# A second accumulator that is added whole to the first, in a scatter-add at the end of a mixture-of-experts layer

## The reference

```python
# layer 0: adaLN, causal attention, dense 8-expert feed-forward; layer 1: adaLN, linear attention, then:
t = rms_norm(xf) * norm_w                                   # 2048 rows
vals, idx = top_k(t @ gate_w.T + gate_b, 4)                 # 16 experts, 4 for each token
G = zeros((M, E)).at[arange(M)[:, None], idx].set(softmax(vals))
h = einsum('mh,eoh->emo', t, w1) + b1
a, b = minimum(h[..., ::2], 7), clip(h[..., 1::2], -7, 7)
y = einsum('emi,edi->emd', a * sigmoid(1.702 * a) * (b + 1), w2) + b2
x = x + gb * (x_in + einsum('me,emd->md', G, y))            # four expert results are added to each token's row
```

## Time and profile before

| | us |
|---|---|
| median of three runs (lowest, highest) | 1005.02 (1004.24, 1008.51) |
| time of the profiled execution | 1002.58 |
| its span, first to last instruction | 1000.8 |
| TensorE busy in it | 969.1 (97%) |
| VectorE busy | 716.9 (72%) |
| ScalarE busy | 673.2 (67%) |
| GpSimd busy | 435.2 (43%) |
| DMA queue of GpSimd (q0): packets' time as a share of 16 engines | 13.7% |
| DMA queue of SyncE (q1) | 44.6% |

### The profile page before, as it was taken

One profiled execution on the slowest core, in us unless ns is written; L12 is line 12 of the kernel. 1 busy time (PEld: TensorE's weight loads), 2 busy tenths in 40 slices (PEclk: granted clock), 3 DMA queues, 4 the chain that ended last, 5 costly groups with the idle time before them and its releaser, 6 DMA issues. The chain is left out here.

```text
span 1000.8 us, 20579 instructions
## 1 busy us (share of the span) xinstructions
PE 969.1 (97%) x6073; PEld 819.3 (82%) x6073; DVE 716.9 (72%) x2499; ACT 673.2 (67%) x1944; POOL 435.2 (43%) x455
## 2 busy tenths in 40 slices
PE   9999999999999999999999999999989989999993
PEld 5769878987887887788789888888768779999992
DVE  4464657767677687768776866785788877888883
ACT  3657778587758757866785776687565647766771
POOL 2322421331263164237225513624137775556876
PEclk9999999999999999999999999999999999999997
DMA  9946993899499421012002001427339789999983
GB/s 316 303 134 219 377 377 125 289 376 376 159 330 376 166 87 54 2 55 87 1 17 104 23 1 41 160 79 270 133 74 249 194 242 254 231 226 235 251 222 63
DMA packets 95517, 182.12 MB, mean 182 GB/s; under 512 B 10237, under 2 KB 30141, under 8 KB 94797
## 3 DMA queue, kind: packets, MB, share of 16 engines
q1 hardware_dynamic: 75243, 149.64, 44.6%
q0 software_dynamic: 18720, 30.79, 13.7%
q10 hardware_dynamic: 1442, 0.38, 0.2%
HBM read 78.22 MB, written 109.56 MB: 188 GB/s over the span
## 5 line engine op out<-in xcount | busy, mean ns | idle before, releaser
L2042 POOL TENSOR_TENSOR RB<-RB 128x512 f32<-128x512 f32 x64 | 66.9, 1045 | 259.4 <-DVE RB L1824 259.3
L1222 PE MATMUL bank<-RB 128*128 128x128 f32 x1264 | 157.1, 276 | 1.8 <-DVE BC L1938 0.7
L1222 PEld LDWEIGHTS bank<-RB 128*128 128x128 f32 x1264 | 149.5, 192 | 4.5 <-DVE BC L1938 1.1
L1505 ACT ACTIVATE RB<-RA,nw 128x512 f32 x158 | 105.4, 714 | 46.8 <-issue 19.8
L1184 PE MATMUL bank<-RA,RB 128*128 128x256 f32 x512 | 133.0, 382 | 2.0 <-ACT RB L1406 2.0
L1156 PE MATMUL bank<-RA 128*128 128x256 f32 x512 | 121.3, 380 | 0.0
L1156 PEld LDWEIGHTS bank<-RA 128*128 128x128 f32 x512 | 95.0, 190 | 15.0 <-issue 3.2
L1184 PEld LDWEIGHTS bank<-RA,RB 128*128 128x128 f32 x512 | 91.2, 190 | 15.9 <-issue 3.0
L2018 POOL TENSOR_TENSOR qs<-qs,half 128x4 f32<-128x4 f32 x64 | 65.5, 1023 | 62.9 <-DVE qs L1833 49.7
L1243 PE MATMUL bank<-RB,BC 128*128 128x256 f32 x316 | 82.0, 383 | 3.2 <-DVE BC L1951 2.8
L1406 ACT ACTIVATE RB<-bank 128x256 f32<-128x256 f32 x128 | 48.6, 380 | 47.8 <-PE bank L1175 46.7
(11 more groups left out here) (263 smaller groups left out, 2394.7 us busy)
## 6 DMA issues: line engine op xcount, KB each, us to landing
xsD<-BC SPq DMA_DIRECT2D x17, 4232.0 KB, 32.8
RB<-in_w2b SPq DMA_DIRECT2D x79, 256.0 KB, 3.8
RB<-xsD SPq DMA_DIRECT2D x68, 264.5 KB, 4.1
BC<-modD SPq DMA_DIRECT2D x16, 512.0 KB, 4.0
RA<-in_w SPq DMA_DIRECT2D x10, 512.0 KB, 6.3
X<-xsD SPq DMA_DIRECT2D x11, 264.5 KB, 3.1
RA<-in_L_attn_Wq SPq DMA_DIRECT2D x2, 1024.0 KB, 10.4
RA<-in_L_attn_Wo SPq DMA_DIRECT2D x1, 2048.0 KB, 17.3
```

The source lines that it names most:

```text
L1222: m = pe.matmul(ps[:, 128 * j:128 * j + 128], WS[:, n % 2, c, 128 * j:128 * j + 128], XT[:, n % 2, c * 128:c * 128 + 128], start=(c == 0), ...
L1505: m = act.activation(WS[:, n % 2, c, :], W1[:, bass.ds(r, 1), c, :].rearrange("p a n -> p (a n)"), ACT.Copy, scale=nw[:, c:c + 1])
L2042: pool.tensor_tensor(sq, qrow, qrow, ALU.mult).then_inc(mine("q_sq", p), 1)
```

## The change

The second accumulator takes blocks 55, 58, 61 and 64 only (before also 67 and 70). Block 67 goes to OUT, blocks 68 to 78 go to ACC (even) and OUT (odd). Behind block 66 (`JOIN`) all rows that ACC2 has, 1280 to 2047 (three batches, 768 KB), are added to ACC in one DMA. It waits for the adds of blocks 64 and 65. Adds to ACC from block 68 on wait for it, and so do the merges of batches 5, 6 and 7. There are eight merges behind blocks (57, 58, 60, 62, 64, 66, 70 and 73) and the same one at the end.

```diff
-THREE, TWO = blocks_with_rows_below(PART), blocks_with_rows_below(NB - 1)
-ADDED_TO = [n % 2 for n in range(THREE)] + [(ACC2, ACC, OUT)[(n - THREE) % 3] for n in range(THREE, TWO)] + [ACC, OUT, OUT, ACC, OUT, ACC, OUT, ACC]
-MERGE_BEHIND = {57: (ACC, 0), 59: (ACC, 1), 61: (ACC, 2), 63: (ACC, 3), 65: (ACC, 4), 66: (ACC, 5), 68: (ACC2, 5),
-                72: (ACC2, 7), 74: (ACC, 6), 76: (ACC2, 6)}
+THREE = blocks_with_rows_below(PART)
+JOIN = 66
+ADDED_TO = [n % 2 for n in range(THREE)] + [(ACC2, ACC, OUT)[(n - THREE) % 3] for n in range(THREE, JOIN + 1)] + [OUT] + [(ACC, OUT)[n % 2] for n in range(JOIN + 2, NBLK)]
+MERGE_BEHIND = {57: (ACC, 0), 58: (ACC, 1), 60: (ACC, 2), 62: (ACC, 3), 64: (ACC, 4), JOIN: (ACC2, NB - 1), 70: (ACC, 5), 73: (ACC, 6)}
...
-                if ADDED_TO[n] == ACC and n > TWO + 1:
+                if ADDED_TO[n] == ACC and n > JOIN:
                     on.wait_ge(*done("merge", ACC2, NB - 1))
...
-                final = blocks_with_rows_below(max(b + 1, PART))
-                target = OUT
-                if (acc, b) == (ACC2, NB - 1):
-                    target, final = ACC, TWO + 1
-                elif acc == ACC2:
-                    on.wait_ge(*done("merge", ACC, b))
-                elif b == NB - 1:
-                    on.wait_ge(*done("merge", ACC2, b))
+                target, final, rows = OUT, blocks_with_rows_below(max(b + 1, PART)), slice(256 * b, 256 * b + 256)
+                if acc == ACC2:
+                    target, final, rows = ACC, JOIN + 1, slice(256 * PART, 2048)
+                elif b >= PART:
+                    on.wait_ge(*done("merge", ACC2, NB - 1))
                 on.wait_ge(*done("y_add", last_added(acc, final)))
                 on.wait_ge(*done("y_add", last_added(target, final)))
```

More of the change, by code:

```diff
@@ L959, in _ @@
             for b in range(NB):
-                on.wait_ge(*done("merge", ACC2 if b in (5, 6) else ACC, b))
+                on.wait_ge(*done("merge", ACC, b))
         @block.tensor
@@ L2110, in merge @@
             def merge(acc, b):
-                final = blocks_with_rows_below(max(b + 1, PART))
-                target = OUT
-                if (acc, b) == (ACC2, NB - 1):
-                    target, final = ACC, TWO + 1
-                elif acc == ACC2:
-                    on.wait_ge(*done("merge", ACC, b))
-                elif b == NB - 1:
-                    on.wait_ge(*done("merge", ACC2, b))
+                target, final, rows = OUT, blocks_with_rows_below(max(b + 1, PART)), slice(256 * b, 256 * b + 256)
[3 more added lines that the diff above has]
+                    on.wait_ge(*done("merge", ACC2, NB - 1))
                 on.wait_ge(*done("y_add", last_added(acc, final)))
                 on.wait_ge(*done("y_add", last_added(target, final)))
-                to_, of = (a[256 * b:256 * b + 256, :].rearrange("(a c) n -> a (c n)", c=8) for a in ((out_r, accD)[target], (None, accD, accE)[acc]))
+                to_, of = (a[rows, :].rearrange("(a c) n -> a (c n)", c=8) for a in ((out_r, accD)[target], (None, accD, accE)[acc]))
                 pool.dma_start(to_, of, accum_op=ALU.add, max_dma_last_dim=8192).then_inc(mine("merge", acc, b), 16)
```

## The result

| | kernel before | changed kernel |
|---|---|---|
| median of 13 runs (lowest, highest), us | 1005.51 (1004.22, 1008.51) | 1008.32 (1005.83, 1010.35) |
| ratio to before, 95% interval | | 1.0023 (1.0013 to 1.0034) |
| the same, a second time (10 and 33 runs) | 1006.18 | 1009.59; 1.0035 (1.0020 to 1.0049) |
| time and span of the profiled execution | 1002.58, 1000.8 | 1005.83, 1004.0 |

The changed kernel is slower by 0.2 to 0.35%, less than the 0.5% that the forecast took as the least that can be told, but with an interval clear of 1. The forecast was 1005.7 from a median of 1005.02. With the ratio of 1.0023 that median gives 1007.3, inside the stated 1002.4 to 1008.2; the median of the 13 runs itself, 1008.32, is just above it.

A forecast was written before the change was run, and what follows sets the result against it. GpSimd's order and the landings it waits for bound the end: block 68 at 971.9 plus 29.6 gives 1001.5, 0.7 us later than 1000.8. So 1002.58 + 0.7 = 1003.3, with 2.4 for the median 1005.7, range 1002.4 to 1008.2.

The forecast's parts named there:

- What bounds the kernel: End of the kernel: the last 15 us are GpSimd's order and the landings it waits for, with TensorE idle.
- Issue of the merge, 962.7: Behind block 66: block 65 added at 956.2, landed 6.2 us later, 768 KB merge issued 0.3 later.
- my upper end for it, 963.7: Latest issue forecast for the 768 KB merge, if GpSimd is a further microsecond late.
- Landing of the merge, 8.3: 768 KB merge behind block 66: 4.8 us as for 256 KB, plus 3.46 for two more thirds of bytes.
- rival 1: 768 KB merge: length costs little, only half of the extra 3.46 us shows; landing 6.5, median 1003.9; chance 0.20.
- Block 68, 971.9: Add of block 68: issued 0.89 us after the merge landed at 971.0, against 964.28 before.
- The way to the end, 29.6: From the add of block 68 to the end of the span: 19.94 + 1.96 + 3.01 + 4.70 us, end at 1001.5.
- I cost this at nothing: Blocks 68 to 78: adds alternating between two tables wait two steps back, 4.08 us covering the landings; cost nothing.
- a gap between blocks 69 and 77 that ends with a DMA: GpSimd's timeline: sign that the forecast is wrong, the thin cover of two tables in turn being gone.
- the floor: Behind block 74: no wait for a merge, two merges fewer; end at 997.15, 3.65 us earlier; as a rival, chance 0.05.
- What the change frees: Block 74 and behind: its wait for a merge and two merges (1.6 us) go; 3.65 us at most.
- Rival 3: 768 KB merge starves behind SyncE's transfers: landing 12.8 us, median 1010.2; landings of 9.5 and more have chance 0.13.

The follow-up runs named there:

- before_again: The kernel before, unchanged, run and profiled once more; ratio to the kernel before 1.0000 (0.9986 to 1.0014).
- spaced: The changed kernel with its first five merges where the kernel before has them (behind 57, 59, 61, 63, 65); ratio to the kernel before 1.0032.
- acc4late: The changed kernel with the merge of batch 4 behind block 67 instead of 64; ratio to the kernel before 1.0014 (0.9997 to 1.0031).
- third: The changed kernel with the merge behind block 66 adding only batch 7, 256 KB instead of 768 KB, output incomplete; ratio to the kernel before 1.0000.
- nojoin: The changed kernel without the merge of 768 KB and every wait for it, output incomplete; ratio to the kernel before 1.0008 (0.9990 to 1.0027).
- nojoin2: The changed kernel without the merge of 768 KB and its waits, run once more, output incomplete; ratio to the kernel before 0.9999 (0.9988 to 1.0011).
- nohold74: The kernel before without the merge of ACC2's batch 7 and the waits for it, output incomplete; ratio to the kernel before 0.9988 (0.9972 to 1.0004).
- third2: The changed kernel with 256 KB instead of 768 KB in the merge behind block 66, run once more, output incomplete; ratio to the kernel before 1.0008.
- again: The changed kernel, unchanged, run once more with a profile of its own; ratio to the kernel before 1.0035 (1.0020 to 1.0049).

## Why the prediction was right in kind and short in size

- *What bounds the kernel*: right. GpSimd's order and the landings it waits for set the end. The last matmul keeps its place; VectorE's last `y_out` moves by 2.4 us, but behind GpSimd, as the prediction had it for block 73.
- *Issue of the merge, 962.7*: it was 964.97. Of the 2.3 us 0.4 is the later start of this execution, 0.7 an add of block 65 that went out later than 956.2, 0.9 its landing, 964.46 - 957.32 = 7.1 us for the 6.2 taken, and 0.2 the 0.5 us from that landing to the merge, for the 0.3 taken. Two programs that are the same up to block 66, before_again and spaced, had this landing at 5.1 and 6.6. This is the largest term that was mis-sized; my upper end for it, 963.7, was too low. It is also as wide as the scatter from execution to execution, so one trace of the kernel before couldn't give it.
- *Landing of the merge, 8.3*: 7.1 and 8.4 in the two profiles, 8.1 and 8.0 in acc4late and spaced. The sum held, though its parts did not quite (packets of about 2.5 us for 3.46), and the 3.3 us between third and the runs with 768 KB let rival 1 fall, which had 1.73 for them. The Trainium skill gives a fit in "DMA: Bandwidth & Descriptors", in its section on the anatomy of a DMA on the software path; an estimate from its slope is 1.2 us for 512 KB, against 3.3 measured. The page doesn't say that the fit holds for accumulating DMAs, and no run here shows what it gives for plain ones.
- *Block 68, 971.9*: 972.96, 1.1 us late. That it came so near is luck: the merge went out 2.3 us later than forecast and landed 1.2 us faster. In the second profile of this kernel the stage started 3.4 us later and block 68 went out 6.1 us later.
- *The way to the end, 29.6*: 1004.0 - 972.96 = 31.0. **The step that failed in its mechanism, and not only in its size, is "I cost this at nothing"**, said of the two tables in turn. Block 70 waited for the landing of 68 (974.90 to 978.02 is 3.12, not 2.04), and block 73 for that of 71 (982.86 to 985.18 is 2.32). The cover was read as 4.08 us against the landing alone. But from the landing to the issue are another 0.84 to 0.86 us, so two steps of 2.04 us cover a landing of 3.2 only; block 68 landed after 4.2 and block 71 after 3.5. The first wait is a gap between blocks 69 and 77 that ends with a DMA, which the prediction had named as a sign of being wrong. Besides, the last add took 3.5 instead of 3.0 us until the last merge. That isn't the two tables: all six runs with a merge behind block 66 have 3.4 to 3.6, nojoin and nojoin2, with the same tables, 3.0. Why is open. The second profile has 1009.8 - 979.01 = 30.8.
- *A step that was not in the sum at all*: block 67 goes to the same table as 66. In the changed kernel it costs nothing, since block 68 waits for the large merge long after 67 is out (966.75, and 972.96); nojoin shows it, at 4.08 us. So even without the large merge this order stays above the floor, by 1.8 us in nojoin.
- *What the change frees*: the hold of block 74 is gone, as said. In the kernel before, nohold74 shows no clear gain from taking that hold away alone (stage 75.0, ratio 0.9988 with an interval that holds 1), since 73 behind 72 in the same table stands right in front of it. The changed kernel has 72 and 73 in different tables, so what the change frees there was not measured alone.
- *Rival 3*, the merge that starves, didn't come: 8.4 us was the longest of the four. The change did what it says.

## What to carry to other kernels

A wait in front of an instruction on an in-order queue costs what everything behind it can't win back: here GpSimd was 8.2 us later than before at block 68 (46.8 against 38.6) and still 2.3 us later at block 78 (69.7 against 67.4), though two merges and a wait were gone in between. When several small accumulations are joined into one, count both landings, that of the last add to the source and that of the join, and look for neighbours that now use the same table. Where the start of a stage scatters by more than the effect, measure from an event inside the stage, profile each kernel more than once, and hold the stages against the timed runs: here they agree on the merge of 768 KB and not on that of 256 KB.

## What the runs showed of the hardware

- From the landing that holds it to its issue, an indirect DMA on GpSimd took 0.84 to 0.89 us, a plain one 0.28 to 0.5 (block 68: merge landed 972.1, add at 972.96; last merge: 0.28 us of issue in the chain; merge of 768 KB in spaced: block 65 issued at 958.89 landed after 6.6 us, merge at 966.00).
- An accumulating DMA between two HBM tables grows by its bytes: at the same place 5.0 and 4.2 us for 256 KB (third, third2) and 7.1, 8.4, 8.1 and 8.0 for 768 KB (changed, again, acc4late, spaced).
- The landing of the add of block 65, 128 rows, varied from 5.1 us (before_again) to 8.2 (third). In before_again SyncE's loads of rows at that time landed after 4.3 us, in spaced, where the add took 6.6, after 7.1. What sets such executions apart is open; none of the runs tells.
